# Opening, chunk spacing and ending of a 64-step gated feed-forward and adapter kernel rearranged

## The reference, cut to what matters

```python
# x (32, 256, 256), cond (32, 64): 32 sequences of 256 rows of 256 numbers
scale = cond @ norm_w.T + 1.0
h = x * (scale[:, None, :] * rsqrt(mean(x * x, -1) + EPS))
val, gate = split(h @ up_w.T, 2, -1)              # up_w (2048, 256)
h = val * gelu(gate)                              # (.., 1024)
y = act_quant(h) @ weight_quant(down_w).T + x     # int8-like rows, ternary weight
# adapter: one pair of 128 x 256 weights per sequence, made from cond
Wd_b = Wd + ((cond @ Wdd.T + bdd) * 0.1).reshape(B, BN, D)
Wu_b = Wu + ((cond @ Wdu.T + bdu) * 0.1).reshape(B, D, BN)
out = y + relu(y @ Wd_b.T + bd) @ Wu_b.T + bu
```

## Time and profile before

| | us |
|---|---|
| median of the 3 runs | 480.48 |
| the profiled execution's own time | 480.89 |
| its span (first to last instruction) | 479.2 |
| PE busy in the span | 467.1 |
| DVE, ACT, POOL busy | 377.8, 365.5, 260.2 |
| mean granted PE clock | 0.995 |

### The profile page before, as it was taken

One profiled execution on the slowest core, in us unless ns is written; L12 is line 12 of the kernel. 1 busy time (PEld: TensorE's weight loads), 2 busy tenths in 40 slices (PEclk: granted clock), 3 DMA queues, 4 the chain that ended last, 5 costly groups with the idle time before them and its releaser, 6 DMA issues.

```text
span 479.2 us, 10039 instructions
## 1 busy us (share of the span) xinstructions
PE 467.1 (97%) x3278; PEld 271.3 (57%) x3278; DVE 377.8 (79%) x789; ACT 365.5 (76%) x636; POOL 260.2 (54%) x676
## 2 busy tenths in 40 slices
PE   8989999999999999999999999999999999999995
PEld 7445656666565455555555555555555555555563
DVE  4798988898898787877877788786777877777776
ACT  5889999999997678768676876867776777777662
POOL 0295775657655446475573746557374543444653
PEclk9999999999999999999999999999999999999997
DMA  7957787777873455565554466455445544544332
GB/s 269 349 113 205 180 244 227 189 210 181 253 176 89 92 121 100 137 147 117 148 133 107 128 141 155 111 153 126 103 136 133 143 103 119 130 123 90 72 85 89
DMA packets 117860, 71.01 MB, mean 148 GB/s; under 512 B 102000, under 2 KB 102960, under 8 KB 115632
## 3 DMA queue, kind: packets, MB, share of 16 engines
q1 hardware_dynamic: 117648, 70.29, 57.2%
q10 hardware_dynamic: 160, 0.07, 0.1%
HBM read 37.44 MB, written 8.39 MB: 96 GB/s over the span
## 4 chain that ended last, share of the span: by engine, by line
PE 88%; DVE 5%; ACT 3%; issue 2%; DMA 1%; POOL 0%; DVEq 0%; ACTq 0%; SPq 0%; POOLq 0%
PE bank L1022 64%; PE bank L1036 11%; PE bank L1113 4%; PE bank L1127 4%; PE bank L1095 4%; PE bank L993 1%; DVE adapt L716 1%; ACT gel L552 1%; DVE xs_lo L746 1%; DMA qT<-qn 1%; DVE hid L767 1%; DVE amax L775 1%; ACT tern L650 0%; ACT qn L574 0%; DVE x L879 0%
## 5 line engine op out<-in xcount | busy, mean ns | idle before, releaser
L767 DVE SCALAR_TENSOR_TENSOR hid<-bank,rms,gel 128x512 f32<-128x512 f32 x127 | 95.2, 750 | 80.4 <-ACT gel L552 79.4
L552 ACT ACTIVATE gel<-bank,rms 128x512 f32<-128x512 f32 x127 | 86.9, 684 | 90.7 <-PE bank L1022 90.6
L1022 PE MATMUL bank<-up_hi,xs_hi 128*128 128x512 f16 x508 | 151.2, 379 | 3.0 <-DVE hid L767 1.5
L1022 PE MATMUL bank<-up_lo,xs_hi 128*128 128x512 f16 x508 | 151.1, 379 | 0.7 <-DVE up_lo L931 0.7
L1022 PE MATMUL bank<-up_hi,xs_lo 128*128 128x512 f16 x508 | 151.1, 379 | 0.0
L1022 PEld LDWEIGHTS bank<-up_lo,xs_hi 128*128 128x128 f16 x508 | 49.6, 98 | 60.9 <-DVE up_lo L931 1.4
L1022 PEld LDWEIGHTS bank<-up_hi,xs_lo 128*128 128x128 f16 x508 | 49.7, 98 | 59.9
L775 DVE TENSOR_REDUCE amax<-hid 128x1 f32<-128x1024 f32 x63 | 76.9, 1220 | 2.2
L565 ACT ACTIVATE hid<-hid,amax 128x1024 f32<-128x1024 f32 x64 | 72.4, 1132 | 2.3 <-DVE amax L781 1.8
L403 POOL TENSOR_TENSOR wsplit<-stage,wsplit 128x288 f16<-128x288 f32 x64 | 52.8, 853 | 34.9 <-ACT wsplit L527 34.9
L1022 PEld LDWEIGHTS bank<-up_hi,xs_hi 128*128 128x128 f16 x508 | 48.3, 98 | 38.5 <-DVE xs_lo L746 2.9
(11 more groups left out here) (129 smaller groups left out, 633.3 us busy)
## 6 DMA issues: line engine op xcount, KB each, us to landing
xT_s<-in_xT SPq DMA_DIRECT2D x32, 256.0 KB, 3.0
xn_s<-in_xn SPq DMA_DIRECT2D x32, 256.0 KB, 3.1
stage<-in_WddT SPq DMA_DIRECT2D x8, 1024.0 KB, 5.4
stage<-in_WduT SPq DMA_DIRECT2D x8, 1024.0 KB, 5.2
out<-out_s SPq DMA_DIRECT2D x31, 256.0 KB, 2.4
adapt<-in_up_wT SPq DMA_DIRECT2D x4, 512.0 KB, 6.8
x<-in_down_wT SPq DMA_DIRECT2D x1, 1024.0 KB, 10.0
qT<-qn SPq DMA_TRANSPOSE x63, 3.1
```

Source lines behind the costliest of these rows:

```text
L552: nc.scalar.activation(gel[:, c], u_gate[c][:], ACT.Gelu, scale=rms[:, t // TPB % XN_SLOTS, t % TPB:t % TPB + 1]).then_inc(gelu_done, 1)
L767: nc.vector.scalar_tensor_tensor(out=hid[:, t % 2, c * 512:(c + 1) * 512], in0=u_val[c][:], scalar=rms[:, t // TPB % XN_SLOTS, t % TPB:t % ...
L1022: ins = nc.tensor.matmul(dst[:], a[:, t // TPB % 2, k, cols], w[:, c, k, v, :], start=(k == 0 and n == 0), stop=(k == KD - 1 and n == 2))
```

## The change

- **Loads.** The first up load is issued first on SP, then x of sequence 0 (its transposed form), the other three up loads, then the rest. cond and norm_w come from ACT's queue. The down weight comes in two halves with a semaphore each. The x of sequence 3 is loaded ahead of the loop. `load_chunk(0)` comes behind base and bias.
- **Tiles 0 and 1.** `up_first(c)` does half c of both tiles: first the eight matmuls per tile that need up_hi, for tile 0 and tile 1, then the four per tile that need up_lo. Tile 1 uses four other banks (`u_banks`). Steps 0 and 1 on PE are `up_first(0)` and `up_first(1)`.
- **xs_hi of sequence 0** is made on the DVE (`first_scaled_high`), no longer on ACT. Fillers are 6 and 4 in place of 8 and 9.
- **Steps 0 to 3** are written out call by call on ACT, DVE and POOL. `rsqrt_first` stands behind the up_lo splits, cond's split in step 2, the three ternary passes in steps 3 and 4 (one to two steps later).
- **Chunks** begin at step 4 and take four steps in five: `CHUNK_STEP` is 4, 5, 6, 7, 9, .., 22. ADAPT[0] is 26, was 21, and adapters follow at five steps for every four sequences until they meet the old timetable 2b + 7.
- **`up`** takes its passes as (hi, up_hi), (hi, up_lo), (lo, up_hi), and waits for xs_lo only at the third; before, each even step began with a wait for it.
- **x1** has 24 slots; norm_w, bias and the identity now lie in other tiles' space.
- **Downs**: down(0) behind up(4, 1), down(1) behind up(5, 0), down(2) behind up(5, 1), then as before.
- **Ending**: see the last part of the diff.

```diff
+def downs(s, c):
+    late = {(4, 1): [0], (5, 0): [1], (5, 1): [2]}
+    return late.get((s, c), [s - DOWN] if c == 0 and s - DOWN >= 3 else [])
+def residuals(s):
+    return {4: [0], 5: [1]}.get(s, [s - DOWN] if s - DOWN >= 3 else [])
 ...
-    return max(2 * b + 7, NGEN + 5 + (4 * b + 2) // 3)
+    return max(2 * b + 7, CHUNK_STEP[-1] + 4 + (5 * b + 2) // 4)
@@ scalar
+            squares(0); scaled_high(1); squares(1); gelu(0, 0); absolute_sum(0); gelu(0, 1)
+            gelu(1, 0); gelu(1, 1); squares(2); gelu(2, 0); quantize(0); quantized(0)
+            gelu(2, 1); absolute_sum(1); scaled_high(2); gelu(3, 0); quantize(1); quantized(1)
+            gelu(3, 1); quantize(2); quantized(2); squares(3)
+            for s in range(FIRST, NT):
 ...
@@ gpsimd
+            rsqrt(1)
+            base_sum()
+            rsqrt(2)
+            for t in range(FIRST - 2):
+                dequantization(t)
 ...
             residual_low(LAST_T - 2)
+            output_bias(B - 2)
             middle_low(B - 3)
-            output_bias(B - 2)
+            pool.wait_ge(x1_lo_done, LAST_T - 2)
+            output_bias_last(1)
             middle_low(B - 2)
-            output_bias_last()
+            output_bias_last(0)
@@ scalar, ending
+            residual_high(LAST_T - 2)
             qT_evacuate()
-            residual_high(LAST_T - 2)
@@ vector, ending
             residual(LAST_T - 2)
+            total(B - 4)
             qT_evacuate()
 ...
-            total(B - 4)
             total(B - 3)
@@ tensor, ending
+            q_transpose()
             down(LAST_T - 1)
-            q_transpose()
             down_last()
 ...
             x_transpose(LAST_T, x63_hi_ps, (0,))
+            middle(B - 2)
 ...
             output(B - 3)
-            middle(B - 2)
             middle_last(1)
```

More of the change, by code:

```diff
@@ L61 @@
 AM_SLOTS = 8
-X1_SLOTS = 20
+X1_SLOTS = 24
 X1N_SLOTS = 4
@@ L640, in _ @@
                                      ).then_inc(up_hi_ready, 1)
-            for s in range(NT):
+            squares(0)
+            scaled_high(1)
+            squares(1)
+            gelu(0, 0)
+            absolute_sum(0)
+            gelu(0, 1)
+            gelu(1, 0)
+            gelu(1, 1)
+            squares(2)
+            gelu(2, 0)
+            quantize(0)
+            quantized(0)
+            gelu(2, 1)
+            absolute_sum(1)
+            scaled_high(2)
+            gelu(3, 0)
+            quantize(1)
+            quantized(1)
+            gelu(3, 1)
+            quantize(2)
+            quantized(2)
+            squares(3)
+            for s in range(FIRST, NT):
                 for b in sequences(s, -1):
@@ L644, in _ @@
                 gelu(s, 0)
[L645 to L653 removed]
+                quantize(s - 1)
                 if s < LAST_T:
@@ L933, in _ @@
                                                ).then_inc(up_ready, 1)
-            for s in range(NT):
+            rsqrt_guess(0)
+            rsqrt_first()
+            scaled_low(1)
+            rsqrt_guess(1)
+            gate(0, 0)
+            gate(0, 1)
+            gate(1, 0)
+            quant_scale(0)
+            gate(1, 1)
+            gate(2, 0)
+            rsqrt_guess(2)
+            quant_scale(1)
+            gate(2, 1)
+            split_cond()
+            quant_scale(2)
+            gate(3, 0)
+            scaled_low(2)
+            ternary_first()
+            gate(3, 1)
+            ternary_second()
+            ternary_third()
+            for s in range(FIRST, NT):
                 if s == LAST_T:
@@ L937, in _ @@
                 gate(s, 0)
-                if s == 0:
-                    scaled_low(1)
-                    rsqrt_guess(1)
-                if s == 2:
-                    ternary_second()
-                    ternary_third()
-                if s >= DOWN:
-                    residual(s - DOWN)
+                if s == FIRST:
+                    quant_scale(3)
+                for t in residuals(s):
+                    residual(t)
                 if s < LAST_T:
@@ L1159, in _ @@
             for s in range(NT):
-                if s % TPB == 0:
-                    pe.wait_ge(xs_done, s // TPB + 1)
+                if s < TPB:
+                    up_first(s)
+                    continue
                 up(s, 0)
-                if s >= DOWN:
-                    down(s - DOWN)
+                if s == 3:
+                    pe.wait_ge(hid_done, NC + 1)
+                    pe.wait_ge(absum_ready, 2)
+                    nc.tensor.matmul(sum_ps, ones[:], wsum[:, 0:1], start=True, stop=False)
+                    nc.tensor.matmul(sum_ps, ones[:], wsum[:, 3:4], start=False, stop=True).then_inc(absum_full, 1)
+                for t in downs(s, 0):
+                    down(t)
                 if s < LAST_T:
@@ L1169, in _ @@
                     up_last(1)
-                if s == 1:
-                    pe.wait_ge(absum_ready, 1)
-                    nc.tensor.matmul(sum_ps, ones[:], wsum[:, 0:1], start=True, stop=True).then_inc(absum_full, 1)
+                for t in downs(s, 1):
+                    down(t)
                 for q in chunk(s, 1):
```

205 lines of the change are left out of this document (118 added, 87 removed).

## The result

The changed kernel takes 482.11 us (median of 11 runs, 481.37 to 483.18), the kernel before 481.1 in the same comparison (11 runs, 479.61 to 481.96). The ratio is 1.0029, 95% interval 1.0017 to 1.004: **slower by 0.3%**, where 475.6 was forecast. The profiled execution took 482.56 with a span of 480.8, against 480.89 and 479.2 before.

A forecast was written before the change was run, and what follows sets the result against it. PE was taken as the bound, busy 97% of the span, so the two ends decide. Gains of 1.7 (start, net), 0.6 (chunks) and 2.6 (ending), 4.9 in all, gave 475.6 us, range 472.5 to 479.0.

The forecast's parts named there:

- Part 1: First two tiles: finished at 17.8 us instead of 21.1, a gain of 3.3 us, bounds 1.7 and 4.5.
- the 4.8 of the first up part: Opening loads: the first up part's best earlier time from issue to landing, 4.8 us with 0.5 MB ahead of it.
- Rival (c): Opening: fewer fillers and a hole run the first two tiles at 1.2 GHz, 10.4 us more, 486.0; chance 0.04.
- nothing was missing in the opening: Argument against a slow opening clock: mean clock 0.995, with the last 25 us at 0.88 alone taking 0.6% off.
- Part 2: Steps 2 to 5: DVE and ACT queues give part back, leaving 1.7 of 3.3 us; bounds -0.3 and 5.9.
- from there it is never idle: DVE in steps 2 to 5: busy without a break after gate(0, 1) at 18.4, until maximum 3 at 36.4.
- Rival (a): Steps 3 to 5: the DVE and ACT queue costs all that the first tiles gain, 477.3; chance 0.15.
- The 0.4 for the ternary weight: PE after up(4, 1): down(0) was to wait 0.4 us for the ternary weight.
- Part 3: Chunks in four steps of five: two xs_lo waits of 0.23 replace one of 1.1, 0.6 us gained.
- the worst case named beside them: Chunk steps: two full waits for xs_lo less the one before, 1.1 us lost.
- Part 4: Ending: reordered last steps on POOL, DVE and PE gain 0.8, 0.4, 1.3 and 0.1, sum 2.6 us.
- the upper bound of 4.0: Ending: the largest gain allowed, if the clock stays up as well, 1.4 us more.

The follow-up runs named there:

- end_passes: Kernel before with the new ending and, in every tile but tile 0, the xs_lo product last of the three: 475.6 us, ratio 0.9905.
- fillers: Changed kernel with twelve units of fillers instead of six ahead of the scale matmuls: 480.57 us, ratio 1.0004 to the kernel before.
- max3_norm_first: max3_first with norm_w's load first on SP, six filler units ahead of the scale matmuls and eleven behind: 473.72 us, ratio 0.9862.
- hid_extra: Changed kernel with hid of tiles 2 and 3 in free slots of x1: 479.16 us, ratio 0.9969 to the kernel before.
- max3_first: hid_every_fillers with tile 3's maximum on the DVE ahead of the second and third ternary pass: 472.93 us, ratio 0.9848 to the kernel before.
- every_step: Changed kernel with a chunk in each of steps 4 to 19, none left out, ADAPT[0] at 23: 480.08 us, ratio 0.998 to the kernel before.
- end_only: Kernel before with the change's new ending and nothing else: 477.35 us, ratio 0.9936.
- hid_every_fillers: Changed kernel with hid of tiles 2 and 3 in x1 slots, a chunk in every step and twelve filler units: 476.53 us, ratio 0.9913.

## Why the prediction was wrong

**Part 1, the opening: 17.8 forecast, 21.49 measured.** The step that failed is "norm_w ... lands between 3.5 and 6.2, I take 4.1". It landed at 6.86, outside the bound: the 4.8 of the first up part was taken as the most that a load beside it could cost, but 64 KB issued behind 512 KB took longer than those. From a first matmul at 9.76, 24 pairs at 0.43 would have ended at 20.1: that is 2.3 of the 3.7 us missed. The other 1.4 are the half rate. The forecast had priced the fillers and the scale matmuls at the slow rate (0.45 a unit, 1.0) and the pairs right behind them at the full one. Rival (c) had the mechanism (the hole and fewer fillers) and gave it 0.04, at 10.4 us for two whole tiles; it came for seven matmuls. Its argument against, "nothing was missing in the opening", was read from the mean granted clock, and that record does not cover an opening: in every trace here PE's first fillers run at half rate (12 in 2.93 us, 16 in 3.78) while it reads 1.00. The kernel before ran so too, up to its first tile matmul at 9.84: 1.06 us for the scale and 4.03 for 18 fillers, against 0.63 and 2.27 at full rate in end_passes. So "no row before shows that at the start" was wrong as well.

The Trainium skill (TensorE: Matmul & The Clock Gate, Part 1) says that half rate is the default and full rate has to be earned by sustained activity. The comparison of fillers with the changed kernel agrees (0.59 against 1.06 for the first pair, with one edit), and so do the other openings: the five executions with six units of fillers and PE idle for 1.15 to 3.01 us ahead of the tiles stayed at half rate until past 12 us, and the four with twelve units were at full rate before norm_w landed. But how much work earns it isn't settled here: the kernel before and end_passes have the same opening, without a stop from 1.28, and reached full rate near 9.8 and by 5.0, and max3_norm_first, without a hole too, still had a first pair of 1.01 at 9.98.

**Part 2, steps 2 to 5: step 6 at 47.0 forecast, 53.06 measured.** 3.7 of the 6.1 were inherited. The failed step is "from there it is never idle" with "PE passes steps 2 and 3 without a stop": the walk counted the DVE's and ACT's durations and left out that hid has two slots, so that gate(2, 0) waits for quantized(0). These waits make 1.34 + 0.93 + 0.33 = 2.6 us, and hid_extra, which takes away that limit alone, gave back 2.95 in the medians. The new order of the opening makes it bite: with both tiles' first halves first, tile 0 is whole only shortly before tile 1. In step 5 the forecast was right: 1.4 for hid and 2.3 for x1 forecast, 1.11 and 1.96 measured, and max3_first showed their cause, maximum 3 behind the ternary passes. The 0.4 for the ternary weight did not come; its passes took 1.2 to 1.3 rather than the 1.45 to 1.7 of before. Rival (a), the start given back whole, is what happened and more, by another mechanism than the one it named.

**Part 3, the chunks: 0.6 gained forecast, 1.15 lost measured.** The two waits for xs_lo came as forecast, 0.2 each; end_passes shows the old one was on the path. The step that failed is the one that left POOL out: the part checked ACT's spare time (0.43 us) and xs_lo, but not POOL's half of a chunk, which generate also waits for and which part 2 had counted for chunk 0. A step without a generate brings PE there 1.4 us sooner, and it waited 0.63, 0.90 and 0.63 us, 2.2 in all, each time until 0.10 us behind POOL's end. every_step, which undoes the gaps alone, gave back 2.0 in the medians and brought these waits down to 0.2. So 2.2 for POOL and 0.5 for xs_lo came in place of 1.1; that the net loss is 1.15 and not 1.6 is some 0.2 us less in every second chunk step than the kernel before took. The loss lies outside the part's bounds, 0 and 1.1 gained; even the worst case named beside them, 1.1 lost, counted full waits for xs_lo, not this.

**Part 4, the ending: 2.6 forecast, 3.8 measured.** Mechanism right, size low. The subtractions gave 0.93 (0.8 forecast), middle(B - 2) went into the hole, and the clock stayed at 1.00 until the end, which the upper bound of 4.0 had for itself. end_only confirms the place. The 3.8 is the difference to an execution in which the clock fell; the medians of end_only give 3.1 to 3.5.

**The sum.** 3.7 + 2.4 + 1.75 - 1.2 = 6.65, against the 6.56 by which the profiled execution (482.56) missed its forecast (476.0). Three terms were too good, and the one that was too poor hid part of it.

## What to carry to other kernels

When a walk moves work forward, write down for each step not only durations but each buffer that it needs back: a two-slot buffer turned an opening that fills PE better into 2.6 us of stalls, and two spare slots took them away. Write down every engine that an instruction waits for, too: a step that gets shorter on one engine runs into the next slowest, here POOL. Where a view says "issue", look at what the program waits for there and when that ended, before putting it down to the engine. Before a small load is moved beside big ones, take its landing as later than that of the big ones, and keep PE at work until it is there (fillers gained 1.2 to 1.5 us by it). And where a change has good and bad parts, run them apart: the ending and the order of the products on the old kernel give 475.6, and the whole change with hid's slots, a chunk in every step, longer fillers and one maximum earlier gives 472.93, where the change as it stood was slower than doing nothing.

## What the runs showed of the hardware

- The record of the granted clock read 1.00 from 10 to 13 us of the changed kernel, while 512-column matmuls started every 0.427 us, twice the time of the later ones. In every trace the opening begins so (16 fillers of 128x128 in 3.78 us from 1.28 on in the kernel before, read as 1.00). A fall later on is on record: 0.50 from 8 to 11 us in hid_every_fillers, behind a hole of 1.74 us. So in an opening the duration of a known matmul tells the rate, and the clock's record doesn't.
- 64 KB issued at 1.37 behind a 512 KB load landed after 5.49 us (5.1 to 6.4 in the other executions with the same loads); issued before the up loads, as in the kernel before, it took 2.1, and first in SP's queue 2.5, but then the first 512 KB part landed 1.4 us later.
- A wait for another engine can be shown as "issue": PE's 0.63 to 0.90 us ahead of a run of 48 small matmuls ended 0.10 us behind POOL's last instruction on their weights, three times out of three.
